# Fused attention and expert-attention layer on one core: ScalarE's filler a slot later, the second bank's copies on VectorE, loops written out

## The reference, cut to what matters

```
x = x + attention1(layernorm(x))          # x: 4 batches x 1024 tokens x 128
x = x + attention2(layernorm(x))

attention1:  q, k, v = projections; 8 heads, each with two maps of width 32
             w1, w2 = softmax(q1 k1^T), softmax(q2 k2^T)      # 1024 x 1024 each
             a = (w1 - lam * w2) @ v                          # width 64
             a = gamma * a / rms(a) * (1 - LAMBDA_INIT);  out = a @ Wout
attention2:  a gate mixes 16 experts' q, k, v projections per token,
             causal softmax attention of width 64, experts' output projections
```

## Time and profile before

| | |
|---|---|
| time, median of 3 runs | 1487.79 us (1487.47 to 1488.07) |
| the profiled execution's own time | 1486.54 us |
| its span, first to last instruction | 1484.8 us |
| busy: PE, DVE, POOL, ACT | 85%, 78%, 74%, 72% |
| granted TensorE clock, mean | 0.962 of full |
| first exp of the first part, last mix | 37.8 us, 1092.3 us |

### The profile page before, as it was taken

How to read it: one execution, slowest core, us unless ns; L and a number is a source line. 1 busy time by engine, 2 the same in 40 slices (tenths; PEclk the granted TensorE clock), 3 DMA queues, 4 the chain that set the end, 5 groups by cost and what they waited for, 6 DMA issues and landing times. The chain is left out here.

```text
span 1484.8 us, 26552 instructions
## 1 busy us (share of the span) xinstructions
PE 1256.0 (85%) x8370; PEld 754.6 (51%) x8370; DVE 1162.6 (78%) x1905; ACT 1071.9 (72%) x1999; POOL 1097.0 (74%) x778
## 2 busy tenths in 40 slices
PE   3788889899988898898989889898863389999997
PEld 1444444444444444444444444444433288989887
DVE  5888888888878887887888788888977366767664
ACT  2888888888878887887888788888743255656553
POOL 3899899989988998998998899999972343433320
PEclk9899999999999999999999999999995599999999
DMA  4231111111211111121111111110003477766670
GB/s 110 71 86 49 40 38 48 35 51 42 54 29 48 48 28 48 32 62 40 48 28 48 48 28 48 39 41 7 1 1 57 92 139 116 128 121 120 121 124 10
DMA packets 184566, 86.33 MB, mean 58 GB/s; under 512 B 150176, under 2 KB 166048, under 8 KB 184480
## 3 DMA queue, kind: packets, MB, share of 16 engines
q1 hardware_dynamic: 184480, 85.33, 26.7%
HBM read 7.68 MB, written 2.10 MB: 7 GB/s over the span
## 5 line engine op out<-in xcount | busy, mean ns | idle before, releaser
L1236 DVE TENSOR_REDUCE negmax<-score_ps 128x1 f32<-128x1024 f32 x512 | 620.8, 1218 | 155.8 <-PE score_ps L602 150.3
L483 POOL TENSOR_TENSOR prob<-prob 128x1024 f32<-128x1024 f32 x256 | 603.6, 2358 | 21.4
L918 ACT ACTIVATE prob<-score_ps,negmax 128x1024 f32<-128x1024 f32 x512 | 571.3, 1116 | 55.1 <-DVE negmax L1236 49.5
L602 PE MATMUL score_ps<-ka,qa 128*128 128x512 f16 x1024 | 314.2, 389 | 127.0 <-ACT prob L918 113.7
L481 POOL TENSOR_SCALAR prob<-prob,ccol 128x1024 f32<-128x1024 f32 x256 | 286.4, 1119 | 73.0 <-DVE ccol L1249 72.5
L625 PE MATMUL trans_ps<-ident,prob 128*128 128x128 f32 x2048 | 276.3, 276 | 3.2 <-POOL prob L483 1.2
L631 PE MATMUL attn_ps<-probT,v_sb 128*64 128x512 f32 x1024 | 277.9, 623 | 1.1 <-DVE probT L327 1.1
L625 PEld LDWEIGHTS trans_ps<-ident,prob 128*128 128x128 f32 x2048 | 242.5, 143 | 63.2 <-DVE probT L327 8.5
L550 POOL TENSOR_TENSOR xs<-xnT,rw_all 128x2048 f32 (+1 forms) x32 | 115.5, 3609 | 171.0 <-DVE prob L1371 164.2
L602 PEld LDWEIGHTS score_ps<-ka,qa 128*128 128x128 f16 x1024 | 75.1, 99 | 282.0 <-ACT prob L918 236.0
L847 ACT ACTIVATE probT<-trans_ps 128x512 f32<-128x512 f32 x320 | 190.8, 597 | 17.9 <-PE trans_ps L625 17.9
(11 more groups left out here) (194 smaller groups left out, 1295.9 us busy)
## 6 DMA issues: line engine op xcount, KB each, us to landing
qa<-split SPq DMA_DIRECT2D x256, 64.0 KB, 2.0
ka<-split SPq DMA_DIRECT2D x256, 64.0 KB, 2.0
xg<-xnT SPq DMA_DIRECT2D x16, 512.0 KB, 3.0
resid<-in_L_attn_x SPq DMA_DIRECT2D x4, 512.0 KB, 6.6
wg<-in_L_attn_Wkv SPq DMA_DIRECT2D x32, 64.0 KB, 2.0
out<-yo SPq DMA_DIRECT2D x32, 64.0 KB, 2.5
wg<-in_L_attn_Wq SPq DMA_DIRECT2D x16, 64.0 KB, 1.8
xsT<-prob SPq DMA_TRANSPOSE x64, 4.5
```

The lines of the kernel that those rows point to most:

```text
L483: pool.tensor_tensor(prob1[:, u, :], prob1[:, u, :], prob2[:, u, :], ALU.add).then_inc(mix_ok, 1)
L602: mm = pe.matmul(score_ps[:, sub, kh * HALF:(kh + 1) * HALF], qa[:, par, head * 2 + sub, q0:q0 + P], ka[:, par, head * 2 + sub, kh * HALF: ...
L918: act.activation(prob2[:, s % 4, :] if sub else prob1[:, s % 4, :], score_ps[:, sub, :], ACT.Exp, bias=negmax[:, s % 2, sub:sub + 1], accu ...
L1236: dve.tensor_reduce(negmax[:, s % 2, sub:sub + 1], score_ps[:, sub, :], AX.X, ALU.max, negate=True).then_inc(max_ok, 1)
```

## The change

Three edits.

1. On ScalarE the block that reads the filler's result is moved. It stood at the end of slot s and read the filler of slot s; now it stands behind the first exp of slot s, ahead of the bank-0 copy, and reads the filler of slot s - 1.
2. ACT_COPIES is gone: VectorE copies bank 1 in every slot, ScalarE never.
3. Every hardware loop (`Fori`) of all five engines is a Python loop, so the instructions are written out. Access patterns and semaphore targets that came from registers are constants.

```diff
-ACT_COPIES = (6, 7, 14, 15)
...
             two_steps(0, True, False)
             sp.wait_ge(ln_late, 6)
-            with sp.Fori(1, ITERS - 1) as it:
+            for it in range(1, ITERS - 1):
                 two_steps(it, False, False)
...
-            with pool.Fori(0, 2) as h:
+            for h in range(2):
                 units(h, False)
-            with pool.Fori(2, 2 * STEPS) as h:
+            for h in range(2, 2 * STEPS):
                 units(h, True)
...
                     if s < SLOTS:
                         softmax(0)
-                    copy_probT(act, act_copy, s, n, it, 0, first, last)
...
-                    if s < SLOTS:
-                        softmax(1)
-                    if s % UNITS in ACT_COPIES:
-                        copy_probT(act, act_copy, s, n, it, 1, first, last)
...
-                    fill = misc_fill(s, first, last)
+                    fill = None if first and s < 1 else misc_fill(s - 1, first, last)
                     if fill and fill[0] in PARTS:
                         part, step = fill
                         proj_copy(part, 2 * it + step, step % 2, "first" if first and step == 1 else "later", misc_ps[:, :])
...
+                    copy_probT(act, act_copy, s, n, it, 0, first, last)
+                    half = half_at(s, ROOT_LAG, first, last)
...
+                    if s < SLOTS:
+                        softmax(1)
...
                     if s + 1 < SLOTS or not last:
                         row_max(n + 1, s + 1, 0)
-                    if s % UNITS not in ACT_COPIES:
-                        copy_probT(dve, dve.tensor_copy, s, n, it, 1, first, last)
+                    copy_probT(dve, dve.tensor_copy, s, n, it, 1, first, last)
```

More of the change, by code:

```diff
@@ L555, in _ @@
             scale_by_experts(1, 1, False)
-            with pool.Fori(1, B * NT // 2) as pair:
+            for pair in range(1, B * NT // 2):
                 scale_by_experts(2 * pair, 0, False)
@@ L689, in _ @@
             slots(0, True, False)
-            with pe.Fori(1, ITERS - 1) as it:
+            for it in range(1, ITERS - 1):
                 slots(it, False, False)
@@ L838, in _ @@
             tiles2(0, True, False)
-            with pe.Fori(1, B - 1) as it:
+            for it in range(1, B - 1):
                 tiles2(it, False, False)
@@ L963, in slots @@
                                        ACT.Copy).then_inc(attn_nT_ok, 1)
+                    copy_probT(act, act_copy, s, n, it, 0, first, last)
+                    half = half_at(s, ROOT_LAG, first, last)
+                    if half is not None:
+                        h = 4 * it + half
+                        act.wait_ge(stat_ok, 2 * (h + 1))
+                        if first and half == 0:
+                            act.wait_ge(rms_least_ok, 1)
+                        act.activation(tl[:, 1, :], tl[:, 0, :], ACT.Ln, bias=rms_least[:, :], scale=RMS_SHIFT).then_inc(root_A, 1)
+                        act.wait_ge(root_A, 2 * h + 1)
+                        act.activation(tl[:, 2, :], tl[:, 1, :], ACT.Exp, scale=-0.5).then_inc(root_A, 1)
+                    if s < SLOTS:
+                        softmax(1)
+                    half = half_at(s, COPY_LAG, first, last)
+                    if half is not None:
+                        act.wait_ge(pv_ok, 8 * (4 * it + half + 1))
+                        if not (first and half == 0):
+                            act.wait_ge(rows_ok, 4 * it + half)
+                        act.activation(attnT[:, :], attn_ps[:, :], ACT.Copy).then_inc(attnT_ok, 1)
                     if last and s - LN2_SLOT - 3 in range(EARLY):
@@ L970, in _ @@
             slots(0, True, False)
-            with act.Fori(1, ITERS - 1) as it:
+            for it in range(1, ITERS - 1):
                 slots(it, False, False)
@@ L1067, in _ @@
             tiles2(0, True, False)
-            with act.Fori(1, B - 1) as it:
+            for it in range(1, B - 1):
                 tiles2(it, False, False)
@@ L1284, in _ @@
             slots(0, True, False)
-            with dve.Fori(1, ITERS - 1) as it:
+            for it in range(1, ITERS - 1):
                 slots(it, False, False)
@@ L1436, in _ @@
             tiles2(0, True, False)
-            with dve.Fori(1, B - 1) as it:
+            for it in range(1, B - 1):
                 tiles2(it, False, False)
```

15 lines of the change are left out of this document (removed).

## The result

The changed kernel takes 1416.24 us (median of 4 runs, 1416.14 to 1416.49), the kernel before beside it 1487.63 (1484.82 to 1488.07): a ratio of 0.9526, 95% interval 0.9511 to 0.954. The profiled execution took 1416.29 us, its span 1414.2, against 1486.54 and 1484.8 before. The forecast was 1429 in a range of 1420 to 1461. So the direction and the main mechanism came true. Between the two profiled executions the span fell by 70.6 us, 11.8 more than the sum of 58.8; the time lies 4 us under the low end of the range.

The account below looks back on a forecast made before the run. GpSimd's own work, 30.8 us a half, was taken as the floor; idle time 49.2 plus back edges 15.6, less 4.5 and 2.5, plus 1.0, gave 58.8 off 1486.54: 1427.7, as a median 1429 us, range 1420 to 1461.

Parts of the forecast that it names:

- the sum of 58.8: Total gain forecast for the whole kernel, in us: 64.8 − 4.5 − 2.5 + 1.0.
- the low end of the range: 1420 us: the forecast with nothing given back (7.0) and the whole 3.1 us in the second part (2.1 more).
- The bound: GpSimd's own work, 30.79 us for eight units, root and norm, is the floor of a half; VectorE's chain needs 29.2.
- The filler: ScalarE's filler one slot later: its waits for TensorE's fillers (35.3 and 30.3 us) go, at no added cost.
- The copies: 64 bank-1 copies of 0.60 us move from ScalarE to VectorE, whose queue of 28.6 us a half stays below GpSimd's.
- The loops: Writing out the 32-slot loops removes five back-edge stalls of 3.1 us in the first part: 15.6 us.
- the second part: One loop back edge of TensorE, ScalarE and VectorE goes there: 0 to 3.1 us, taken as 1.
- The sum 49.2 + 15.6 = 64.8: GpSimd's idle time removed over 30 halves (1.64 us each) plus the back edges removed, in us.
- Given back, 7.0 us: GpSimd held by L1277, 0.15 us in each of 30 halves (4.5), and two halves until it has its backlog (2.5).
- Rival 1: GpSimd stays locked to L1277, held by the addition of unit 3: 1.20 us a half stay, 1458 us; chance 0.26.
- Rivals 2 and 3: First: straight code stalls like the loop, 1444 us, chance 0.09. Second: VectorE's 64 copies lie on the chain, 1511, 0.07.

Follow-up runs that it names:

- run 5: The changed kernel with GpSimd's addition covering only half of each unit's 1024 columns (not the reference's attention): 1373.47 us.
- run 3: The changed kernel with ScalarE's filler put back in its old slot, behind the second exp: 1469.64 us.
- run 2: The changed kernel with bank 1 of four slots in sixteen copied by ScalarE again, not by VectorE: 1416.29 us.
- run 1: The kernel before with all loops written out, filler and copies as before: 1469.58 us.
- run 4: The changed kernel with its loops kept, filler and copies moved: 1419.47 us.
- run 6: The changed kernel with VectorE's small eps operation one place earlier in its queue, between the two row maxima: 1415.37 us.
- run 9: The changed kernel with GpSimd's root as four scalar_tensor_tensor operations in one VectorE slot, the reciprocal placed as in the changed kernel: 1447.09 us.
- run 10: The kernel of run 9 with the 64 bank-1 copies back on ScalarE: 1434.21 us.
- runs 7 to 10: The changed kernel with GpSimd's root on VectorE, over two slots, then in one, each with copies on VectorE, then ScalarE: 1440.70, 1434.15, 1447.09, 1434.21 us.
- runs 11 and 12: The kernels of run 9 and run 10 with the eps column computed by ScalarE instead of VectorE: 1412.58 and 1397.47 us.

## Why the prediction was right, and where not

**The bound.** Right. GpSimd's half of 30.79 us was the floor: 30.72 measured, and with less work on GpSimd the time falls at once (run 5). The chain of the others was put at 29.2 and is 29.48 (run 5).

**The filler.** Right: it carries the gain. Without it nothing beyond the loops is left (run 3). Its cost on ScalarE, 0, holds: TensorE's transposes wait mostly for GpSimd's addition, and no row shows them waiting for a copy of ScalarE's.

**The copies.** Right, and exactly: nothing, on either engine, with the chain or GpSimd as the bound (runs 2 and 3).

**The loops.** The 3.1 us for each back edge are right for the kernel before (run 1: 17.0 us with the second part). The sum 49.2 + 15.6 = 64.8 is right only as a sum, GpSimd's idle time. Its split is not what the parts are worth: with the filler moved, the loops bring 3.2 us (run 4). Had the loops stayed, the same method would have forecast some 1445, and the time is 1419. The Trainium skill (Runtime: NRT & Kernel Launch, Instruction fetch mechanics) says that a taken branch breaks sequential prefetch and can stall its engine. The runs agree as far as they go, with 3.1 us at each back edge of the 32-slot loops and none in straight code; that the time is spent on fetching is not shown. The prediction's sentence that by this rule the 15.6 us are gained in full holds for run 1 alone.

**Given back, 7.0 us: this step failed.** The prediction had GpSimd lose 0.15 us in each half to the passage of L1277 and 2.5 us until it has its lead. The trace has GpSimd held up by next to nothing: even with the operation held in every half (run 6) a half grows by 0.05 us, and in the changed kernel L1273 comes at a boundary and the half is no longer than GpSimd's own work. The prediction also let VectorE arrive earlier and earlier until it is held. It doesn't: from the sixth half to the last three the leads of the eight units repeat within some 0.1 us. The trace shows what ties them: TensorE's transposes wait for GpSimd's addition, and VectorE's row maximum for the scores behind them, so VectorE's queue keeps its phase to GpSimd's. What the two early holds (1.39, 0.59 us) cost GpSimd is one idle time of 1.20 us, at 115.72. On the whole 67.0 us of idle time were removed; the forecast had 64.8 − 7.0 = 57.8. This makes 9.2 of the 11.8 us.

**The rest.** GpSimd's own work is 1.9 us shorter, about the 2.2 us by which its halves are longer with the loops kept (run 4), which the prediction had at nothing; why they are is open, since the turn of GpSimd's loop takes 3.54 us either way. The second part, 1.9 in place of 1.0, makes 0.9; the other rows of the table make −0.2.

**The low end.** It was set by taking back the 7.0 us and adding 2.1 for the second part. It left no room for GpSimd's own work to shrink (1.9 us), nor for the idle time beyond the 64.8 us to go, of which 2.2 went. The two are the 4 us that were missing. Two smaller terms cancel: the second part gave 1.9 of the 3.1 us allowed for it, and the 1.25 us from the profiled execution to the median, which the forecast added, didn't come again (1416.29 and 1416.24).

**The rivals.** Rival 1 was the right danger with the wrong condition. It doesn't hang on the phase at which VectorE arrives, as the prediction worked out with a margin of 0.4 to 0.5 us, but on the lead. As long as VectorE's queue with its holds is shorter than GpSimd's half, GpSimd has 2.6 us and more in hand and a hold of 1.8 us is absorbed: by the timelines VectorE is idle for 1.7 us of a half in the changed kernel and for 0.45 in run 6, so there its queue fills 30.3 of the 30.77 us. If the queue is the longer one there is no lead, the hold lands on GpSimd, and the period stays locked: in run 9 VectorE is idle for 0.25 us of a half of 31.89 (run 10 has the same idle time for the column). What the earlier trace rows show are two halves without a lead, and no lock: the operation comes 0.80 us behind the addition's start in one and 0.14 in the next, since that addition starts at 1072.17. What limits this account is that the lead and VectorE's queue were never varied without moving other operations too. Why the operation settles just at the boundary in the changed kernel, rather than near it, stays open. It isn't chance: in run 2 (204.35 and 204.39) and run 4 (205.23 and 205.29) it settles there too. Rivals 2 and 3 are out by runs 1 and 3.

## What to carry to other kernels

Gains of several edits against one bound don't add: take each alone down to the floor, and count the idle time of the binding engine once. Read how far ahead of the binding engine its inputs are, not only whether it waits: with a lead, stalls and held operations cost next to nothing, and without one a 0.16 us operation can cost 1.20 us in each round. Work taken off the binding engine can lengthen the chain of the engine that receives it, by its own time and by its holds: the root moved to VectorE cost 18 to 31 us (runs 7 to 10), and brought 3.7 and 18.8 only when another held operation had been taken off VectorE (runs 11 and 12).

## What the runs showed of the hardware

Some of VectorE's small operations are held until the end of the GpSimd operation in progress, whichever of its two large ones it is. In the changed kernel L1273 at 143.50 took 0.59 us, and the scaling that had begun at 142.94 with 1.12 us had 0.56 left; in run 9 it took 1.86 us with 1.84 of the addition left. The prediction had seen it only for additions. In the 28 halves in which L1273 came some 0.05 us behind the start of a scaling, and so at the end of the addition before it, it was not held (0.16 to 0.18 us). The scaling's row in the changed kernel's timeline of GpSimd, and the one idle time that a hold (of L1273 at 113.16) cost there:

```profile
115.72 1.12 POOL L480 TENSOR_SCALAR prob<-prob,ccol 128x1024 f32<-128x1024 f32 x1 [1.20 <-DVE ccol L1246]
...
142.94 1.12 POOL L480 TENSOR_SCALAR prob<-prob,ccol 128x1024 f32<-128x1024 f32 x1
```

Held were, with all operands in SBUF, the on-chip memory, tensor_scalar with a constant, tensor_tensor and scalar_tensor_tensor. Not held were the reciprocals (145 to 164 ns, 256 of them in the changed kernel), the tensor_scalar of one column with scalars from memory (272 to 277 ns) and the reduction beside it (671 to 687 ns, 32 of them). The Trainium skill (SBUF — State Buffer, Who interferes with whom) says that a VectorE operation in a two-port mode contends with GpSimd, one with two inputs from SBUF contends with a GpSimd operation that reads SBUF, and a tensor_reduce never does. The trace agrees, for the scaling (0.59 us) as for the addition (1.86 us).

A back edge of the 32-slot loops costs 3.1 us where GpSimd has nothing ready; where it has, in run 4, it shows as a late column (5.35 us in place of 4.1) and not in GpSimd's scalings.
